# Counting candidates in eight products of 120 columns in place of four of 240

## What is computed

```python
def balanced_assignment(scores):          # T = 8192 tokens, E = 8 experts, C = 1024
    taken = jnp.zeros((T,), dtype=bool)
    for e in range(E):
        s = jnp.where(taken, -jnp.inf, scores[:, e])
        _, idx = jax.lax.top_k(s, C)
        parts.append(idx)
        taken = taken.at[idx].set(True)
    return jnp.concatenate(parts)

scores = norm @ centroids.T
routed = feat[balanced_assignment(scores)].reshape(E, C, D)
h = layer_norm(routed, ln_g, ln_b)
h = gelu(einsum('ecd,edf->ecf', h, w1) + b1)
out = routed + einsum('ecf,efd->ecd', h, w2) + b2      # and back to the tokens' places
```

## Time and profile before

| | |
|---|---|
| median of 3 runs | 1338.49 us (1336.6 to 1339.36) |
| profiled execution | 1338.32 us, its span 1336.5 us |
| busy: TensorE products | 1045.8 us (78%), 14370 of them |
| busy: VectorE | 843.7 us (63%) |
| busy: GpSimd | 741.4 us (55%) |
| count products (L1309) | 448, 84.2 us busy |

### The profile page before, as it was taken

One profiled execution on the slowest core, in us unless ns is written; L12 is line 12 of the kernel. 1 busy time (PEld: TensorE's weight loads), 2 busy tenths in 40 slices (PEclk: granted clock), 3 DMA queues, 4 the chain that ended last, 5 costly groups with the idle time before them and its releaser, 6 DMA issues. The chain is left out here.

```text
span 1336.5 us, 36666 instructions
## 1 busy us (share of the span) xinstructions
PE 1045.8 (78%) x14370; PEld 725.1 (54%) x14370; DVE 843.7 (63%) x2718; ACT 665.9 (50%) x1388; POOL 741.4 (55%) x683
## 2 busy tenths in 40 slices
PE   0499999999999976359999960739995547999993
PEld 0155556565656543136777750728884214777772
DVE  4267777777777657788886105675665788888400
ACT  0277777777777745603323320846774732223340
POOL 0288888888888850026777781003441004777886
PEclk9999999999999988559999985878997757999997
DMA  6000000000000004502333335000001621334333
GB/s 179 16 3 3 3 3 3 3 3 3 3 3 3 3 3 129 160 16 49 58 60 62 76 36 134 0 0 1 1 2 41 180 69 28 54 57 74 60 61 30
DMA packets 82886, 56.01 MB, mean 42 GB/s; under 512 B 13472, under 2 KB 74144, under 8 KB 82720
## 3 DMA queue, kind: packets, MB, share of 16 engines
q1 hardware_dynamic: 60192, 36.92, 9.9%
q0 software_dynamic: 22528, 16.79, 9.4%
HBM read 28.53 MB, written 25.17 MB: 40 GB/s over the span
## 5 line engine op out<-in xcount | busy, mean ns | idle before, releaser
L510 DVE TENSOR_TENSOR patt_aa<-p_second_aa,first_aa 128x512 f32<-128x512 f32 x320 | 205.9, 685 | 124.7 <-ACT first_aa L442 75.2
L1393 POOL DMA_INDIRECT rows_e<-norm_rows,index_e x128 | 127.6, 997 | 240.5 <-DVE index_e L1109 202.7
L373 POOL TENSOR_TENSOR patt_aa<-patt_aa,causal_aa 128x512 f32<-128x512 f32 x192 | 240.7, 1280 | 34.9 <-DVE patt_aa L510 34.9
L442 ACT ACTIVATE first_aa<-p_first_aa 128x512 f32<-128x512 f32 x320 | 173.8, 595 | 113.7 <-PE p_first_aa L617 113.5
L617 PE MATMUL p_first_aa<-q_t_aa,k_t_aa 32*128 32x256 f32 (+2 forms) x1280 | 188.0, 444 | 8.5 <-ACT first_aa L442 8.5
L617 PE MATMUL p_second_aa<-q_t_aa,k_t_aa 32*128 32x256 f32 (+2 forms) x1280 | 192.7, 444 | 0.0
L1231 PE MATMUL p_h_e<-rows_t_e,w_e 128*128 128x512 f32 x256 | 136.2, 648 | 0.2
L1241 PE MATMUL p_y_e<-w_e,hid_e 128*128 128x128 f32 x1024 | 135.3, 275 | 0.0
L1309 PE MATMUL p_cnt_e<-reach_e,ones_e 128*128 128x240 bf16 x448 | 84.2, 319 | 63.9 <-DVE reach_e L1155 63.9
L617 PEld LDWEIGHTS p_first_aa<-q_t_aa,k_t_aa 32*128 32x128 f32 (+1 forms) x1280 | 85.3, 162 | 84.6 <-ACT first_aa L442 42.9
L1360 ACT ACTIVATE hid_e<-p_h_e,b_e 128x512 f32<-128x512 f32 x128 | 88.0, 687 | 79.2 <-PE p_h_e L1231 78.8
(11 more groups left out here) (266 smaller groups left out, 2124.6 us busy)
## 6 DMA issues: line engine op xcount, KB each, us to landing
norm_rows<-norm_n SPq DMA_DIRECT2D x32, 256.0 KB, 2.3
w_e<-L_ffn_w SPq DMA_DIRECT2D x32, 256.0 KB, 2.9
ffn_rows<-x SPq DMA_DIRECT2D x8, 512.0 KB, 3.2
x<-ffn_rows SPq DMA_DIRECT2D x8, 512.0 KB, 7.3
out<-x SPq DMA_DIRECT2D x8, 512.0 KB, 3.2
rows_e<-norm_rows,index_e POOLq DMA_INDIRECT x128, 2.5
b_e<-L_ffn_b SPq DMA_DIRECT2D x16, 64.0 KB, 3.8
ffn_rows<-yb_e,index_e POOLq DMA_INDIRECT x64
```

Of the source, the lines that this page charges most:

```text
L373: pool.tensor_tensor(unit, unit, seen, ALU.mult).then_inc(masked, 1)
L442: act.activation(first[group(g, n) % 2][:, b, :], p_first[b][:], ACT.Identity).then_inc(first_copied, 1)
L510: dve.tensor_tensor(patt[of % LAG][:, b, :], p_second[unit % ROOMS][:], first[of % 2][:, b, :], ALU.mult).then_inc(patt_done, 1)
L1393: pool.indirect_dma_start(rows[lpar][:, j, :], None, norm_rows, bass.IndirectOffsetOnAxis(ap=list_of(l, lpar)[:, j:j + 1], axis=0)).then_i ...
```

## The change

The products of a pass are cut in half: eight of 120 columns (15 candidates x 8 tiles), four per half of the tiles, where there were four of 240. Which of them wait stays as it was, the first of each half. All eight are added to the first 120 columns of `p_cnt`, and VectorE's sum (whose code is the same, but for the value of SPAN) reads 120 columns, eight for each candidate, in place of 16.

```diff
-    SPAN = TILES // 4
+    SPAN = TILES // 8
+    SPANS = TILES // SPAN
...
-                        for q in range(TILES // SPAN):
-                            if q % 2 == 0:
-                                pe.wait_ge(reached, 2 * PASSES * e + 2 * n + q // 2 + 1)
-                            mm = pe.matmul(p_cnt[:, 0:SPAN * CANDS], ones[:],
-                                           reach[:, q // 2, :, (q % 2) * SPAN:(q % 2 + 1) * SPAN],
-                                           start=(q == 0), stop=(q == TILES // SPAN - 1))
+                        for q in range(SPANS):
+                            side, first = q * 2 // SPANS, q % (SPANS // 2) * SPAN
+                            if first == 0:
+                                pe.wait_ge(reached, 2 * PASSES * e + 2 * n + side + 1)
+                            mm = pe.matmul(p_cnt[:, 0:SPAN * CANDS], ones[:], reach[:, side, :, first:first + SPAN], start=(q == 0), stop=(q == SPANS - 1))
```

## The result

The changed kernel takes 1330.46 us in the median of 4 runs (1329.85 to 1331.17); the kernel before, run beside it, 1338.01 us (4 runs, 1336.6 to 1339.36). The ratio is 0.9944, 95% interval 0.9927 to 0.9961, faster by 7.55 us. The forecast was 1331.1 us. The profiled execution took 1331.17 us with a span of 1329.1, so 7.4 us less than before.

What follows compares the result with a forecast made beforehand. The bound was a ring between VectorE and TensorE, with 64 sums on the chain of waits. 64 x 0.125 us less 0.57 us for products gave 7.43 us, so 1331.1 us; forecast's own range 1328.5 to 1334.5.

Steps and rivals of the forecast that it cites:

- The sum: VectorE's sum in each pass, 120 columns in place of 240: 283 ns from 408, a saving of 125 ns.
- the 105 ns: Lower end of the saving per sum, if part of the price is per result: 6.15 us in all, 1332.3 us.
- 32 sums per layer: Sums on the chain of waits: 8 + 8 + 5 + 3 x 3 + 2 over searches 0 to 6; 64 in both layers.
- The pace of the products: TensorE's products of 120 columns start 52.6 ns apart at full clock; at half clock eight cost what four cost.
- The rival of loads that set the pace: TensorE's products wait for whole weight loads, 101 ns each at full clock: slower, 1355 us; chance 0.08.
- that of no change: Products about 80 ns apart at full clock, nothing more at half clock: gain and loss cancel, 1338.5 us; chance 0.10.
- 17 ns for a group in one piece: A pass's eight products on TensorE at full clock, issued in one piece: 421 ns where four need 404.
- 8 ns for that of pass 7: Added time of pass 7's products at full clock, where only the second half lies behind the last comparison.
- the three sums: Sums of passes 1, 2 and 6 on the chain in a full-clock search: 3 x 125 ns saved, less 76 for products.
- the 1.3 us per layer: Most lost if TensorE's clock rise in search 2 stays in time while the work comes 2.6 us earlier.
- The full-clock searches give nothing back: Rival: TensorE or ScalarE covers their three sums too; only 5.25 us gained, 1333.2 us; chance 0.08.
- all 112 sums count: Rival: every sum of the kernel sets the time, 112 x 0.125 = 14.0 us gained, 1324.5 us; chance 0.04.

Runs made afterwards that it cites:

- the delays: Changed kernel plus a dummy VectorE instruction behind the sum, searches 3 to 6: in passes 1, 2 and 6, 1333.57 us; in passes 0, 3, 4, 5 and 7, 1330.69.
- the last count product is long: Six products of 120 columns and a last one of 240 per pass, sum over 240, candidates with two table inputs; 1334.97 us, 0.998 to the kernel before.
- the other form: Changed kernel with the candidate instruction written with two table inputs in place of table plus numbers; 1327.17 us, ratio 0.9921 to the kernel before.
- the sixteen products: Changed kernel cut further, SPAN at TILES // 16: sixteen products of 60 columns, sum over 60; 1327.59 us, 0.992 to the kernel before.
- the kernel before with the other form: Kernel before (four products of 240 columns, sum over 240) with the candidate instruction written with two table inputs; 1334.44 us, ratio 0.998.
- 40 delays in the covered passes: Changed kernel plus a dummy instruction behind the sum in passes 0, 3, 4, 5 and 7 of searches 3 to 6; 1330.69 us, ratio 0.9946.

## Why the prediction was right, and where its sum was off

- **The sum.** Forecast 283 ns from 64 to one (225) and 240 to 15 (408); 282 measured. With 60, 30, 120 and 240 columns at 220, 189, 282 and 408 all lie on 158 ns plus 1.04 ns per element, and so does that of 64 to one result with 225, so the row of 64 to 16 out of SBUF was the wrong neighbour and the 105 ns fell.
- **32 sums per layer.** Right: searches 0 and 1 lost 8 x 0.126 us (0.91 in one of four), and the delays show passes 1, 2 and 6 at full clock and no others.
- **The pace of the products.** Forecast 52.6 ns at full clock by the line through 64 and 240 columns, 52.5 measured; at half clock in proportion, 100 measured. The rival of loads that set the pace fell with it, and so did that of no change: they needed 80 ns and more. The Trainium skill's 81 ns for a sustained stream at 128 columns (page "TensorE: Matmul & The Clock Gate", section "Back-to-back issue gap") didn't hold for these eight in a row. The formula that the same section of the Trainium skill gives for a product by itself makes, as an estimate, 52.5 ns of 120 columns, which is what was measured.
- **The step that failed: 17 ns for a group in one piece, 8 ns for that of pass 7, and that what waits behind the products starts later only by these.** The group costs 10 ns. I had left out the first product behind it: with eight, the second record behind the group starts 49 ns later against the first, which goes again when the last count product is long, so I put it down to the float32 load that lost 50 ns of its cover. That makes 59 ns behind passes 0 and 1 and about 55 behind pass 7, of which 0.12 us show in a search, not 0.076 (0.04 of it stays when the last product is long, and its cause open). With the three sums, that makes 0.375 - 0.12 = 0.25 us for searches 3 to 5; without hold-ups 0.21 to 0.26 were measured. Of the missing 0.54 us this is 0.37 (2.24 to 1.87).
- **Not foreseen: the candidate's hold-ups.** I wrote that VectorE and GpSimd issue the same in the same order, which is so, but their place against each other moved. In the changed kernel pass 2 is held up by 0.08 us in six full-clock searches, and pass 4 by 0.35, covered; net of what the searches give back elsewhere, that is, by what the other form gives, the other 0.17 us (1.87 to 1.70). In search 2 it went the other way: the hold-up of 0.21 us in pass 1 is gone, and that pass is shorter by 0.44 and 0.27 us where a sum alone gives 0.13. That is the gain beyond the forecast there; pass 7, with four up products behind it, took 0.11 of it back. Of the 0.44 some 0.1 us stays unexplained.
- **The clock.** Its rise came 4.02 us earlier in the first run and 7.44 in the second, and the work there 3.13 and 6.55, so it came 0.9 us earlier in the work, in pass 5 of search 2 as before. Passes 5 and 6 show no gain or loss beyond the sum's, so the 1.3 us per layer that I allowed were not needed here. The term is real, though: where the rise came in pass 6 (first run of the sixteen products, second run of the kernel before with the other form), that pass took 1.1 to 1.3 us longer. That it cost nothing here is luck. Why it rises when it does, no run shows. (The 1334.5 at the top of the forecast's own range doesn't come out of its working: 2 x 1.3 above 1331.1 is 1333.7, above the 1332.3 it is 1334.9.)
- **The full-clock searches give nothing back** and **all 112 sums count** both fell: 0.08 to 0.29 us per search arrived, and 40 delays in the covered passes made the searches that hold them 0.05 us longer in all.

## What to carry to other kernels

Cutting a product in two along its columns and adding the halves in PSUM moves a sum from VectorE (1.04 ns per element) to TensorE almost for nothing as long as the pieces stay above the floor, here some 26 ns at full clock; but look at the load of the instruction behind the last piece: here a shorter last piece made what follows 49 ns later, and at full clock a second halving gained next to nothing. When a change shifts VectorE against GpSimd's transfers, look for instructions whose maximum is far above their median, and try another form of them that reads the same data.

## What was not expected of the hardware

The candidates written with two table inputs take 220 and 281 ns where the form with numbers takes 253 and 311, and stay at that 430 to 800 ns into GpSimd's gathers, where the form with numbers was held up by 75 to 221 ns (in a scatter by up to 354); but those that began between 23 ns ahead of a gather and 10 ns into it took 23 to 54 ns more, and one that began 95 ns ahead of a gather took 345 ns in place of 281. The form with numbers wasn't held up where it began 10 to 400 ns into a gather. A float32 load of 190 ns behind a product of 120 columns delays the second record behind it by 49 ns against one of 240 columns, by 73 ns behind one of 60 (192 ns between the two records of the first down product) or of 30 (192 again). And products of 30 columns, each with its own load of 97 ns, start 26 ns apart at full clock: four such loads are under way at once in the records.
